# Gate weight transposes moved from the last pair stage of a batch to its second, their loads a batch ahead

## What is computed

```
x = x + tanh(g_xattn[0]) * cross_attention(layernorm(x), ctx)      # 16 heads of 64, 256 context rows and a null key, then a layernorm
x = x + tanh(g_ffn[0])   * ffn_quantized(layernorm(x))             # relu, hidden 1024, 8-bit float rounding
x = x + tanh(g_xattn[1]) * depool(layernorm(x), ctx)               # matrix product and a decaying scan of the context
x = x + tanh(g_ffn[1])   * mixture_of_experts(layernorm(x))        # 8 experts, the best 2 of them, gelu(gate0) * gate1, hidden 512
```

## Time and profile before

| | |
|---|---|
| median of 3 runs | 1606.15 us |
| the profiled execution's own time | 1607.19 us |
| its span in the trace | 1605.4 us |
| TensorE matmul (PE) busy | 1462.8 us, 91% |
| VectorE (DVE) busy | 1201.3 us, 75% |
| ScalarE (ACT) busy | 921.9 us, 57% |
| GpSimd (POOL) busy | 635.4 us, 40% |
| mean granted TensorE clock, share of full | 0.968 |

### The profile page before, as it was taken

The page is one execution under the profiler, slowest core; times in us unless marked ns, Lnnn a source line. Parts: engine busy times, 40 slices in busy tenths (PEclk is TensorE's granted clock), DMA queues, the critical chain, the costliest instruction groups (busy, mean ns, idle before and its releaser), DMA issues.

```text
span 1605.4 us, 36164 instructions
## 1 busy us (share of the span) xinstructions
PE 1462.8 (91%) x12542; PEld 1077.5 (67%) x12542; DVE 1201.3 (75%) x3252; ACT 921.9 (57%) x2526; POOL 635.4 (40%) x774
## 2 busy tenths in 40 slices
PE   3999999999999999999999999999765499999997
PEld 2667676767767677777767676777653266666665
DVE  6578889898988889898988889898873354545543
ACT  4476766767677676767676676767651133333332
POOL 5302242434243342424244243424424355555554
PEclk7999999999999999999999999999977699999999
DMA  8102022020202012020202102010400373333332
GB/s 264 66 1 67 15 67 68 13 80 2 80 8 74 30 52 80 2 80 2 80 15 67 59 22 80 2 60 8 171 34 7 103 181 55 55 55 59 58 60 31
DMA packets 77599, 92.90 MB, mean 58 GB/s; under 512 B 21248, under 2 KB 61200, under 8 KB 77424
## 3 DMA queue, kind: packets, MB, share of 16 engines
q1 hardware_dynamic: 50912, 72.69, 13.7%
q0 software_dynamic: 15680, 17.78, 6.8%
q10 hardware_dynamic: 10832, 0.13, 0.4%
HBM read 60.70 MB, written 30.78 MB: 57 GB/s over the span
## 4 chain that ended last, share of the span: by engine, by line
PE 54%; DVE 30%; ACT 8%; issue 3%; DMA 2%; POOL 1%; ACTq 0%; SPq 0%; POOLq 0%; DVEq 0%
PE S L1373 11%; PE W L1031 8%; PE W L1033 8%; PE W L1032 8%; DVE mx L1562 6%; PE T L1036 6%; PE O L1393 6%; ACT prob L860 3%; DVE pTl L1574 3%; PE O L1138 3%; PE S L1110 2%; PE W L1036 2%; DVE st_ln L1533 1%; DVE nm L1565 1%; DVE xh L1543 1%
## 5 line engine op out<-in xcount | busy, mean ns | idle before, releaser
L860 ACT ACTIVATE prob<-S,nm 128x256 f32<-128x256 f32 x512 | 235.5, 474 | 82.6 <-DVE nm L1565 82.4
L681 POOL TENSOR_SCALAR ve_ln<-mv_ln 128x2 f32<-128x2 f32 x64 | 14.3, 223 | 542.8 <-DVE mv_ln L1536 542.7
L853 ACT ACTIVATE pTh<-T 128x512 f16<-128x512 f32 x256 | 139.4, 597 | 111.7 <-PE T L1036 111.7
L1373 PE MATMUL S<-GL,xgh 128*128 x568 | 170.1, 381 | 2.8 <-DVE xgl L1870 2.8
L1574 DVE SCALAR_TENSOR_TENSOR pTl<-T,pTh 128x512 f16<-128x512 f32 x256 | 164.0, 680 | 7.3 <-ACT pTh L853 7.2
L1562 DVE TENSOR_REDUCE mx<-S 128x2 f32<-128x512 f32 x256 | 163.1, 678 | 8.0 <-PE S L1110 8.0
L777 POOL DMA_INDIRECT out_dram<-ysb,tab x71 | 112.1, 1579 | 132.2 <-issue 86.6
L869 ACT ACTIVATE prob<-prob,rden 128x256 f32<-128x256 f32 x256 | 116.2, 501 | 71.6 <-DVE p0n L1583 71.6
L1036 PE MATMUL T<-ident,prob 128*128 128x128 f32 x1024 | 141.6, 282 | 1.5 <-DVE prob L1589 1.4
L1031 PE MATMUL W<-cTh,Wkh 128*128 128x256 f16 x512 | 140.5, 274 | 0.0
L1032 PE MATMUL W<-cTl,Wkh 128*128 128x256 f16 x512 | 140.4, 274 | 0.0
(11 more groups left out here) (300 smaller groups left out, 4367.9 us busy)
## 6 DMA issues: line engine op xcount, KB each, us to landing
cx<-in_ctx_dram SPq DMA_DIRECT2D x16, 512.0 KB, 5.1
gst<-in_L_ffn_gating_w_dram SPq DMA_DIRECT2D x16, 512.0 KB, 6.3
gating_split<-gsp SPq DMA_DIRECT2D x16, 512.0 KB, 2.7
GL<-gating_split SPq DMA_DIRECT2D x8, 1024.0 KB
stg<-in_L_xattn_Wkv_dram SPq DMA_DIRECT2D x8, 512.0 KB, 13.5
xl<-in_x_dram SPq DMA_DIRECT2D x16, 256.0 KB, 4.0
lst<-in_L_ffn_linear_w_dram SPq DMA_DIRECT2D x16, 256.0 KB, 5.2
xres<-in_x_dram SPq DMA_DIRECT2D x16, 256.0 KB, 2.8
```

Of the source, the lines that this page charges most:

```text
L853: A(flat(pTh[:, h, :, :]), T[h][:, :], ACT.Copy).then_inc(s_pTh[h], 1)
L860: ins = A(prob[:, h, t, :], S[h][:, t * NTOK:(t + 1) * NTOK], ACT.Exp, bias=nm[:, h, t:t + 1], scale=SM, accum_out=rs[:, h, t:t + 1])
L1373: ins = M(o[:, :], (xgl if n == 2 else xgh)[i % 2][:, k, :], GLflat[:, bass.ds(w, HID)], start=(k == 0 and n == 0), stop=(k == KD - 1 and ...
```

## The change

The two gT units are named in `UNITS` between the first `k` and the first `q` instead of before `rank`. PE makes them in stage 1, behind `values(0)` and before the wait for `xT`. ScalarE copies their high halves in stage 1 behind `norm(1)`, and VectorE takes the low halves behind `add_residual`. SP writes `gsp` out ahead of the rows of stage 7, and directly behind that write it loads the slice of the next step into `gst`; only the first slice is still loaded at the start of step 0.

```diff
 UNITS = [("ctxT", True, PRE), ("ctxT", True, PRE), ("wout", False, POST),
-         ("xT", True, PRE), ("k", True, PRE), ("q", True, PRE), ("q", True, PRE),
+         ("xT", True, PRE), ("k", True, PRE), ("gT", True, ATTN), ("gT", True, ATTN), ("q", True, PRE), ("q", True, PRE),
          ("k", True, PRE), ("x1T", True, POST), ("q", True, PRE), ("q", True, PRE), ("s0", False, PRE),
...
          ("v", True, PRE), ("v", True, PRE), ("x4T", False, POST), ("logits", False, POST),
-         ("gT", True, ATTN), ("gT", True, ATTN), ("rank", False, POST)]
+         ("rank", False, POST)]
@@ SP, step
                     sp.dma_start(lst[:, :, :], pick(lin_v, i.n)).then_inc(s_lw, 16)
-                    sp.dma_start(gst[:, :, :], pick(gat_v, i.n)).then_inc(s_gw, 16)
+                    if i.n == 0:
+                        sp.dma_start(gst[:, :, :], gat_v[0]).then_inc(s_gw, 16)
...
-                if POST in parts:
-                    rows_out(i, post, work)
                 if ATTN in parts:
                     for k, nfull, _ in work.at["gT"]:
                         wait_apart(sp, free[k], nfull)
                     sp.dma_start(pick(gsplit_d, i.n), gsp[:, :, :, :].rearrange("p a b c -> p (a b c)"))\
                       .then_inc(s_go, 16)
+                    if i.n + 1 < NB:
+                        sp.dma_start(gst[:, :, :], gat_v[i.n + 1]).then_inc(s_gw, 16)
+                if POST in parts:
+                    rows_out(i, post, work)
+                if ATTN in parts:
                     wait_apart(sp, s_lsp, i.n + 1)
@@ ScalarE, j == 1
                         if attn:
                             norm(j)
+                            at_least(act, s_go, 16 * i.n)
+                            for m in range(2):
+                                one("gT", m, gsp[:, 0, m, :], WS)
                         if pre:
                             q_high(0)
                             q_high(1)
@@ ScalarE, j == 7
                             prob_high(j)
-                            at_least(act, s_go, 16 * i.n)
-                            for m in range(2):
-                                one("gT", m, gsp[:, 0, m, :], WS)
                             attn_high(3)
@@ TensorE, j == 1
                     if attn and j:
                         values(j - 1)
+                    if j == 1 and attn:
+                        gating_units()
                     if j == 1 and pre:
                         evicted("xT")
                         q_unit(0)
@@ TensorE, j == 7
                         if post_:
                             logits_unit()
                         if attn:
-                            gating_units()
                             values(j)
@@ VectorE, j == 1
                         if post_:
                             add_residual()
+                        if attn:
+                            for m in range(KD):
+                                low("gT", m, gsp[:, 1, m, :], gsp[:, 0, m, :], WS)
                         if pre:
                             q_low(0)
                             q_low(1)
@@ VectorE, j == 7
                             select()
-                        if attn:
-                            for m in range(KD):
-                                low("gT", m, gsp[:, 1, m, :], gsp[:, 0, m, :], WS)
                         if post_:
                             take_ranks()
```

## The result

The change made the kernel slower: 1640.17 us (median of four runs, 1638.81 to 1644.32) against 1605.87 us (1604.9 to 1606.67), a ratio of 1.0218 with a 95% interval of 1.0199 to 1.0238. The forecast was 1636.4, range 1620 to 1648. The profiled execution took 1644.32 us, the longest of the four; its span is 1642.6 us, 37.2 more than before. TensorE (PE) is busy 1473.8 us of it and the instruction counts are the same.

The account below looks back on a forecast made before the run. PE, busy 1462.8 of 1605.4 us, was taken to bound the kernel. Fourteen full steps (27.9), step 0 (2.4) and step 15 (0) sum to 30.3 us, giving 1636.4 on the median 1606.15; range 1620 to 1648.

Parts of the forecast that it names:

- Stage 7 gives PE nothing: Stage 7: the removed transposes (1.00 us) lay in a wait, so removal gives 0.00 us at `rank` and `scores(0)`.
- VectorE 0.74 ahead: From stage 7 on: without its gT low halves (1.28 us), VectorE starts `aTl` at 630.35, not 631.09, and runs 0.74 us ahead.
- The banks of q 0 and q 1: Stage 1: `q` 0 waits for `k` 0's bank (0.9 us idle), `q` 1 for gT 0's (1.1); `scores(2)` 1.99 us later.
- The ledger: Check on the step's cost: PE gets 0.9 us work, 0.9 + 1.1 idle, and loses waits of 0.59, 0.29 and 0.17.
- The same cost in every full step: Steps 1 to 14: each full step costs 1.99 us, 27.9 us for 14.
- Nothing made up later: Stage 2 to stage 7: PE has no other wait to make up the 2 us; rival, half comes back, 1621, chance 0.11.
- The hq wait: PE's next wait after stage 1 (0.51 us): hangs on `maxima(3)` behind the `q` halves and moves along.
- The ends: First and last steps: step 0 costs +2.4 us; step 15 taken as 0, of -1.95 to +1.28.
- The clock: Stage 1: rival that two PE standstills of about 1 us drop the clock every full step, 23.5 us more, 1660; chance 0.05.
- The 12 us at 0.99: Evidence against the clock drop: granted clock held at 0.99 over 12 us with PE busy only 5.78.

Follow-up runs that it names:

- Experiment 2: Kernel before the change, each gT unit made by one short matmul of zeros from step 1 on, in stage 7: 1606.45 us.
- experiment 8: Kernel before the change, VectorE taking only 32 of 512 columns of each low half of gT in steps 1 to 15: 1596.61 us.
- experiment 3: Changed kernel, each gT unit made by one short matmul of zeros in stage 1, in steps 1 to 15: 1643.63 us.
- experiment 4: Changed kernel, VectorE taking the two low halves of gT ahead of `add_residual` in stage 1: 1629.74 us.
- experiment 10: Changed kernel, `place()` of VectorE (routing records) moved from stage 0 to stage 3: 1630.69 us.
- experiment 5: Changed kernel, gT low halves ahead of `add_residual`, k 0's low half ahead of `divide(1)`, ScalarE's gT copies ahead of `norm(1)`: 1625.4 us.
- experiment 6: Changed kernel, eight transposes of the identity that nobody reads put into stage 7: 1634.84 us.
- experiment 7: Changed kernel, gT and k 0 evictions moved earlier on VectorE and ScalarE, plus eight unread transposes in stage 7: 1617.65 us.
- experiment 9: Kernel before the change, `place()` of VectorE (14 small operations for routing records) moved from stage 0 to stage 3: 1593.4 us.

## Why the prediction was right

**Stage 7 gives PE nothing: right.** `rank` starts 1.57 us behind `values(7)` in the trace after (572.76 to 574.33) and 1.56 before. Experiment 2 shows the same by itself.

**VectorE 0.74 ahead: right.** It reads the bank of `wout` 12.22 us behind `scores(0)`, where it was 12.94: 0.72 ahead. In experiment 8 the same relief gave 0.71 a step.

**The banks of q 0 and q 1: right**, to 0.02 us. Counted from `scores(0)`, the low half of k 0 was forecast to end at 15.27 us and ended at 15.29; q 1 at 17.77 and 17.78; `scores(2)` at 19.18 and 19.19. (The ledger that the prediction calls in agreement gives less: 0.9 + 0.9 + 1.1 - 0.59 - 0.29 - 0.17 is 1.85, not 1.99.) Experiments 3 and 4 show that the bank's eviction is the cause and the amount of work isn't.

**The same cost in every full step: not in step 1.** It costs 2.57 us. VectorE has no records to place there yet, and before the change its stages 0 and 1 were already 7.45 and 8.92 us long (7.82 and 9.37 in later steps), so the relief had less to take away.

**Nothing made up later: nearly right.** A full step costs 1.83 and not 1.99. From `scores(2)` to `scores(3)` it was 9.12 before and is 8.70: two short hand-offs from VectorE that no row names shrank by 0.42. Stage 3 is 0.24 longer, for hq. The hq wait didn't only move along, as the text had it. This term was 14 x 0.16 = 2.2 us too large.

**The ends.** Step 0 was forecast at +2.4 and is +2.7. Step 15 with what follows was taken at 0 with an upper bound of 1.28 and is +2.7, of which 2.0 are for the low clock in its stage 0. That fall begins at the end of stage 7 of step 14, as the three others do at the ends of steps 1, 8 and 11.

**The clock: the step that failed.** The rival stood at 0.05, located in stage 1 and taken as all or nothing. In the trace the clock falls at the end of stage 7 in four full steps of fourteen, and three full steps and step 15 pay some 2 us each for it. What the text missed is that taking the transposes out of stage 7 leaves PE with 0.84 and 0.72 us of standing still close together, with 0.85 us of value products between. Its evidence against was also misread. The 12 us at 0.99 in the earlier trace rows end where the clock falls, and the clock was low ahead of them too, as the windows on both sides in the same trace show (columns as in the earlier trace rows):

```profile
1164.00:1168.00 4.00, 2.93 (x20) 2.12 (x21) 2.18 (x8) 3.17 (x12) 3.33 (x4) 0.60 0.00 0
...
1182.00:1186.00 4.00, 4.00 (x25) 2.70 (x25) 1.19 (x3) 1.39 (x3) 0.00 (x0) 0.59 0.00 0
```

So the kernel before already had a low clock beside idle PE in step 15, and the window didn't show that such idle time is harmless.

**How the number came to fit.** That the forecast lies only 4 us below the median is partly luck. On the profiled execution it was 30.3 us against 37.2: 2.2 too much for the steps, against 5.7 + 2.0 too little for the clock, 0.7 for step 1 and 0.7 for the rest of step 15. The median is 4.2 us below the profiled execution; why isn't known, since the other runs left no trace and their mean clocks (0.963 and 0.964) aren't above its 0.968.

The Trainium skill's rule on this ("TensorE: Matmul & The Clock Gate", section "A second HAM failure mode: psum-queue depth-cycling"), that short idle spells between matmul groups can make the clock swing, was set aside on the strength of one window. The trace after agrees with it in kind: a clock of 0.50 at 722 to 724 us, in a fall that begins during the second of two waits below 0.9 us.

## What to carry to other kernels

A unit that is put into a rotation of banks changes who waits for whom: find for every unit behind it which eviction now frees its bank, and read when that eviction comes in the evicting engine's program, not how long it is. Here that was 1.83 us a step, and a swap of two calls gave half of it back. Work that lies in the wait of a saturated engine is free there and may keep its clock up; the busiest engine's share (91%) doesn't tell what a step waits for, since some 0.4 us less on PE gave nothing and 1.2 us less on VectorE, at 75%, gave 0.71.

## What the runs showed of the hardware

The granted clock fell to the lower of its two levels (1.2 instead of 2.4 GHz) in some full steps and not in others of the same program, and then at the same place, between 0.8 us before the end of stage 7 and 0.7 us behind it: four times in the changed kernel (behind steps 1, 8, 11 and 14) and in experiments 3 and 10, five times in experiments 2, 4 and 5, never in the kernels with the gap filled (6, 7). PE had stood still twice just before, for 0.84 and 0.72 us, in experiment 2 for 0.40 and 0.72. In the kernel before and in experiments 8 and 9, where only the wait of 0.71 us stands there, no full step had a low clock. The one fall of a full step at another place is that of step 1 in experiment 6.

In the changed kernel such a fall makes stage 0 some 2.9 us longer and stage 1 1.0 shorter, because PE comes later to its wait there: 1.9 us net. In experiment 10 it is 1.1 net. In experiment 2 it is nothing: stage 0 is up to 1.2 us longer, and PE's waits in stages 1 and 2 give all of it back.

The spread of the times proves little on this: 5.5 us over four runs of the changed kernel and 1.8 over four of the kernel before, but 4.8 over nine and over nineteen other runs of the kernel before, and 5.2 with the gap filled.
